# Self-attention with the values as stationary operand, probabilities divided by their sums before they are turned, and units of two even and two odd heads

## The chip, the cores and the metric

The kernel runs on one core of a Trainium2 chip. The time is device time of one execution, in microseconds (us). TensorE is called PE here (PEld are its weight loads), VectorE is DVE, ScalarE is ACT, GpSimd is POOL, and SP issues DMAs.

## What is computed

A decoder of seven stages on x of 32 samples, 112 rows and 256 columns, all in fp32. The change touches the first stage alone, self-attention with 8 heads of 64 columns on the normalised x:

```python
qk = x @ W_qk + b_qk
q, k = (qk[..., 0], qk[..., 1])
v = (x @ W_v + b_v).reshape(b, s, H, D_HEAD)
sim = jnp.einsum('bihd,bjhd->bhij', q, k) * scale
attn = jax.nn.softmax(sim, axis=-1)
o = jnp.einsum('bhij,bjhd->bihd', attn, v)
y = _layernorm(o @ W_out + b_out, ln_gamma, ln_beta)
return (y + x) * RSQRT2
```

The six stages behind it (projection of a context, two cross-attentions, two mixtures of experts, a gated attention) are the same before and after.

## The kernel before

`self_attention` (line 449) works in eight **groups** of four samples. Each sample is two **units** (u = 0 to 7 in a group, 64 in all); a unit is four heads, the even ones of a sample in an even unit and the odd ones in an odd unit. The order of work on each engine is written out by hand in `group` of that engine (PE line 613, ACT 676, DVE 761). Engines wait for each other by counting semaphores, and each engine works strictly in its own order. The first and the last group are written out; the six between run in a loop, where the values waited for are worked out in registers.

What a unit goes through, step by step:

- PE `scores` (L573): four matmuls of 64 rows by 112 columns, in one PSUM bank for even units and another for odd ones. Even heads stand in partitions 0 to 63 of qT and kT, odd heads in 64 to 127. A unit before uses one of the halves.
- DVE `shift`: the maximum over the keys (L727) and the subtraction (L730).
- ACT `exp` (L662).
- PE `turn_prob` (L582): four transposes of the probabilities; ACT `copy_probT` (L667) brings them to SBUF.
- PE `values` (L593): probT is stationary (112 columns), v moving (64 columns and one of ones, which gives the row's sum).
- DVE `normalise`: reciprocal of that sum (L737) and the product (L740), into `sa_o`.
- once per sample, PE `turn_out` (L602, four transposes of `sa_o`), ACT `copy_oT` (L673), PE `project` (L609, four matmuls of 256 columns), DVE `keep_y` (L747 to L751: bias and statistics).

In unit u PE does: turn_prob(u), scores(u + 1), a job of the next group, values(u), a second job, then `turn_out` of the sample before where u is even and `project` where u is odd. The jobs (`PLAN`, line 458) make the next group's operands: the transposes of x in u = 1, q and k in u = 2 to 5, v in u = 6 and 7. The last group has no jobs. DVE normalises the next group's x (`norm`, L708) at the start of unit 0, and takes the statistics of the context (`context_stats`, L758) in even units. The next unit's turn_prob needs the probabilities of u + 1, so scores, shift and exp of u + 1 run while PE does the rest of unit u.

Of the kernel before, what the change touches and what calls it, by code (L numbers as in the profile page):

```python
# [448 lines left out]
def self_attention(e):  # L449
# [5 lines left out]
    SCORE = (bank[0], bank[1])  # L455
    TURNED, PV, OT, Y = bank[2], bank[3], bank[6], bank[7]
# [6 lines left out]
    with ExitStack() as st:  # L463
# [12 lines left out]
        v = sb("sa_v", [T, 2, GROUP, H, HD + 1])  # L476
# [3 lines left out]
        rinv = sb("sa_rinv", [T, 2, HU])  # L480
        o = sb("sa_o", [T, 2, H, HD])
# [19 lines left out]
        rinv_done = count("sa_rinv_done")  # L501
        o_ready = count("sa_o_ready")
        oT_ps, oT_ready = count("sa_oT_ps"), count("sa_oT_ready")
# [16 lines left out]
        with nc.Block() as block:  # L520
# [9 lines left out]
            def _(pe):  # L530
# [33 lines left out]
                def scores(g, r, u):  # L564
                    s, odd = divmod(u, 2)
# [4 lines left out]
                    for i in range(HU):  # L570
                        h = 2 * i + odd
                        p0 = HD * odd
                        last = pe.matmul(SCORE[odd][0:T, i * T:(i + 1) * T],  # L573
                                         qT[p0:p0 + HD, r, h // 2, s * T:(s + 1) * T],
                                         kT[p0:p0 + HD, r, h // 2, s * T:(s + 1) * T], start=True, stop=True)
# [9 lines left out]
                def values(g, r, u):  # L585
                    s, odd = divmod(u, 2)
# [10 lines left out]
                def turn_out(g, s):  # L597
                    pe.wait_ge(o_ready, ONE + g * UNITS + 2 * s + 2)
                    pe.wait_ge(oT_ready, ONE + g * GROUP + s)
                    ov = o[:, s % 2].rearrange("t h e -> t (h e)")  # L600
                    for k in range(4):
                        last = pe.transpose(OT[:, k * T:(k + 1) * T], ov[:, k * P:(k + 1) * P], ident[0:T, 0:T])  # L602
                    last.then_inc(oT_ps, 1)
# [1832 lines left out]
```

## Time and profile before

| | us |
|---|---|
| median of 3 runs | 3142.16 |
| lowest and highest run | 3135.05 and 3143.45 |
| the profiled execution | 3136.99, its span 3135.2 |
| attention part of the stage, first turn_prob to last matmul | 73.72 to 473.96 |

Over the whole span PE is busy for 88%, DVE 48%, ACT 36%, POOL 20%; the granted clock of PE is 0.91 of full speed on average. In rows of busy time by stretch the columns are: the stretch, its length, busy us of PE, PEld, DVE, ACT and POOL (with their records), PE's granted clock, the DMAs' share and GB/s. Times in rows are us from the start of the span, those called "mean" are ns. PE prints an fp32 matmul as two records and a transpose as one, so a unit's four score matmuls are x8. A record is longer than the distance to the next, since matmuls are pipelined: what a step costs PE is the distance from its start to the next step's start. Clock 1.00 stands for TensorE at 2.4 GHz, 0.50 for 1.2 GHz.

### The profile page before, as it was taken

The page shows a single profiled execution, that of the slowest core. Times are in us where ns is not written, and L with a number is a line of the kernel's source. Part 1 is how long each engine was busy: PE and PEld are TensorE (multiplying, and loading weights), DVE is VectorE, ACT ScalarE, POOL GpSimd, SP SyncE. Part 2 cuts the span into 40 slices and gives each one's busy share as a digit, 9 for nine tenths or more (in the row PEclk, how much of TensorE's full clock was granted, in tenths as well). Part 3 has the DMA queues.
Part 4 walks back from the last instruction along what each step waited for, and adds up shares of the span by engine and source line. Part 5 has one row for each costly group of instructions (what it writes and reads, how often), then busy time and mean ns, then how long its engine had stood idle before and what let it go on. Part 6 is the DMA issues. An engine that isn't in the chain of part 4 may idle for free. (4 is left out here: it accounts for less than half of the span.)

```text
span 3135.2 us, 58175 instructions
## 1 busy us (share of the span) xinstructions
PE 2746.9 (88%) x19352; PEld 2247.6 (72%) x19352; DVE 1498.8 (48%) x3187; ACT 1113.3 (36%) x2348; POOL 638.5 (20%) x660
## 2 busy tenths in 40 slices
PE   4999994996999998499999969899789999849992
PEld 2767672674888887488888857666578888848882
DVE  3455556335767664500000036555567777553334
ACT  1222235332555553033333324332145555402220
POOL 0000000003333331022222200000143333104542
PEclk8899996997999997599999989999889999859996
DMA  5000001786777772255655668600168888415666
GB/s 135 23 23 22 22 22 31 245 283 164 191 189 190 188 191 66 67 176 177 207 178 194 202 195 296 224 1 1 42 157 210 204 204 205 111 35 183 206 212 195
DMA packets 284132, 459.92 MB, mean 147 GB/s; under 512 B 73234, under 2 KB 211956, under 8 KB 284004
## 3 DMA queue, kind: packets, MB, share of 16 engines
q1 hardware_dynamic: 267236, 408.97, 46.0%
q0 software_dynamic: 16768, 49.30, 4.8%
q8 instruction: 72, 1.18, 0.2%
q14 instruction: 56, 0.46, 0.0%
HBM read 339.13 MB, written 119.02 MB: 146 GB/s over the span
## 5 line engine op out<-in xcount | busy, mean ns | idle before, releaser
L1389 ACT ACTIVATE x_probT<-banks 125x448 f32<-125x448 f32 x768 | 418.0, 544 | 402.3 <-PE banks L1292 392.6
L1495 DVE TENSOR_REDUCE x_neg_max<-banks 112x2 f32<-112x750 f32 x512 | 455.8, 931 | 97.7 <-PE banks L1276 97.7
L2000 PE MATMUL banks<-f_xT,f_w 128*128 128x256 f32 (+1 forms) x1680 | 368.7, 376 | 24.5 <-DMA f_b<-in_L_ffn_b 9.7
L2000 PEld LDWEIGHTS banks<-f_xT,f_w 128*128 128x128 f32 x1680 | 310.0, 196 | 76.6 <-issue 11.6
L1433 POOL TENSOR_TENSOR x_diag<-ident,x_neg_max 112x448 fp32r<-112x448 f32 x256 | 240.8, 941 | 575.4 <-DVE x_neg_max L1495 553.5
L2012 PE MATMUL banks<-f_w,f_hT 128*128 128x256 f32 x1584 | 354.3, 380 | 0.0
L1290 PE MATMUL banks<-x_diag,x_ones 112*125 112x448 f32 x768 | 324.5, 423 | 10.5 <-POOL x_diag L1433 9.8
L2012 PEld LDWEIGHTS banks<-f_w,f_hT 128*128 128x128 f32 x1584 | 296.2, 191 | 37.5
L1292 PEld LDWEIGHTS banks<-x_qP,x_kP 128*125 128x125 f32 x1536 | 291.3, 190 | 14.9
L1292 PE MATMUL banks<-x_qP,x_kP 128*125 128x224 f32 x1536 | 291.5, 271 | 0.0
L1276 PE MATMUL banks<-x_kP,x_qP 128*112 128x376 f32 x1024 | 264.5, 341 | 10.4 <-DMA x_qP<-q_halves 9.6
L2059 DVE TENSOR_TENSOR f_y<-banks,f_b 128x256 f32<-128x256 f32 x66 | 25.1, 420 | 478.2 <-PE banks L2012 478.2
L1940 POOL DMA_INDIRECT y_rows<-f_y,f_goes x132 | 131.2, 994 | 463.7 <-DVE f_y L2059 338.3
L2034 ACT ACTIVATE f_hT<-banks,f_b 128x256 f32<-128x256 f32 (+1 forms) x280 | 126.0, 461 | 219.7 <-PE banks L2000 202.2
L1308 PE MATMUL banks<-x_probT,x_v 125*32 125x112 f32 x6144 | 200.5, 263 | 0.8 <-ACT x_o4T L1397 0.8
L1931 POOL DMA_INDIRECT f_x_slots<-x_rows,f_came x132 | 130.2, 986 | 250.2 <-POOLq L101 198.7
L1290 PEld LDWEIGHTS banks<-x_diag,x_ones 112*125 112x125 f32 x768 | 143.8, 187 | 41.9 <-ACT x_probT L1389 22.0
L1308 PEld LDWEIGHTS banks<-x_probT,x_v 125*32 125x32 f32 x6144 | 138.7, 109 | 30.2 <-ACT x_o4T L1397 1.2
L1276 PEld LDWEIGHTS banks<-x_kP,x_qP 128*112 128x112 f32 x1024 | 147.9, 180 | 12.8 <-issue 10.1
L2037 ACT ACTIVATE f_hT<-banks 128x256 f32<-128x256 f32 (+1 forms) x140 | 52.0, 371 | 189.4 <-PE banks L2000 188.4
L949 PE MATMUL banks<-p_ctxT,x_wk_by_head 128*128 128x375 f32 x256 | 91.3, 501 | 27.2 <-DMA p_ctxT<-in_ctx_T 20.4
L2051 DVE TENSOR_TENSOR f_hT<-f_hT 128x256 f32<-128x256 f32 (+1 forms) x140 | 57.4, 410 | 90.7 <-ACT f_hT L2037 89.3
(321 smaller groups left out, 4096.7 us busy)
## 6 DMA issues: line engine op xcount, KB each, us to landing
x_kP<-k_halves SPq DMA_DIRECT2D x512, 188.0 KB, 3.6
f_w<-in_L_ffn_w SPq DMA_DIRECT2D x70, 1024.0 KB
f_w<-in_L_ffn_w SPq DMA_DIRECT2D x70, 512.0 KB
x_qP<-q_halves SPq DMA_DIRECT2D x512, 56.0 KB, 3.2
x_v<-v_rows SPq DMA_DIRECT2D x64, 408.0 KB, 3.2
k_halves<-p_halves SPq DMA_DIRECT2D x32, 752.0 KB, 3.6
k_halves<-f_d_halves SPq DMA_DIRECT2D x32, 752.0 KB, 4.0
q_halves<-x_q_halves SPq DMA_DIRECT2D x64, 224.0 KB, 2.3
```

The lines of the kernel that those rows point to most:

```text
L1276: last = pe.matmul(bank[2 * pair + k][0:T, 0:NKV + 1], qP[:, s, k, 2 * q + pair, :], kP[:, r, 2 * q + pair, :], start=True, stop=True)
L1290: pe.matmul(to, ones[:], diag[:, u % RING].rearrange("t h k -> t (h k)"), start=True, stop=False)
L1292: last = pe.matmul(to[:, 2 * pair * T:2 * (pair + 1) * T].rearrange("k (h t) -> k h t", t=T), kP[:, r, 2 * q + pair, keys], qP[:, s, :, 2 ...
L1308: last = pe.matmul(PV[j * VW:(j + 1) * VW, 0:T], v[0:KB, s % 2, at:at + VW], probT[:, u % 2, c, j, :], start=(c == 0), stop=(c == NJ - 1))
L1389: act.activation(probT[:, u % 2, c].rearrange("k h t -> k (h t)"), ST[i % 2][0:KB, 0:HU * T], ACT.Exp).then_inc(exp_done, 1)
L1433: pool.tensor_tensor(diag[:, u % RING], wide(ident[0:T, 0:T].unsqueeze(1), 1, HU), wide(mx[:, u % RING, :].unsqueeze(2), 2, T), ALU.mult). ...
L1495: dve.tensor_reduce(mx[:, u % RING, 2 * pair:2 * pair + 2], psum[0:T, 2 * pair:2 * pair + 2, 0:NKV], AX_X, ALU.max, negate=True).then_inc( ...
L1931: pool.indirect_dma_start(out=x_slots[:, n % 2, j, :], out_offset=None, in_=e.x_rows, in_offset=bass.IndirectOffsetOnAxis(ap=came[:, at:at ...
L1940: pool.indirect_dma_start(out=e.y_rows, out_offset=bass.IndirectOffsetOnAxis(ap=goes[:, at:at + 1], axis=0), in_=y[:, n % 2, j, :], in_off ...
L2000: last = pe.matmul(bank[1 + f % 3][:, 0:width], w1[:, r, k, f * P:(f + 1) * P], xT[:, r, k, 0:width], start=(k == 0), stop=(k == KD - 1))
L2012: last = pe.matmul(bank[4 + 2 * r + j][:, 0:D], hT[:, f, j * P:(j + 1) * P], w2[:, r, f, :], start=(f == 0), stop=(f == NF - 1))
L2034: act.activation(hT[:, f, 0:width], bank[1 + f % 3][:, 0:width], ACT.Gelu, bias=b1[:, r, f:f + 1]).then_inc(h_raw, 1)
```

## The change

- **Units** take another four heads: both even and both odd ones of half a sample (`part` 0 and 1), issued by turns: even, odd, even, odd. The scores of even heads go to bank 0, those of odd heads to bank 1, and the part selects columns 0 or 256 of both. DVE reads both banks with one instruction.
- **values** has v as the stationary operand (64 columns) and probT moving (112 columns). The output is already turned: an even head lands in PSUM partitions 0 to 63 and an odd one in 64 to 127, in two banks used by turns. `turn_out` and its semaphores are gone. ACT copies 128x224 a unit (`copy_oT`, once a unit in place of 128x448 once a sample).
- **The division** is done on the probabilities: `normalise` is gone, and DVE's new `weigh` takes the sum of each row (112x448 to 112x4), its reciprocal, and the product over 112x448, between exp and turn_prob. turn_prob waits for `weighed`, not for `exp_done`.
- **Order**: DVE does shift(u + 1), context_stats where u is even, weigh(u + 1), jobs, keep_y. ACT does copy_probT(u), exp(u + 1), copy_oT(u - 1), jobs. PE does `project` of the sample before in even units. v has no column of ones.

The core of the diff (renamed counters and declarations left out):

```diff
     SCORE, SCW = (bank[0], bank[1]), 256
@@ scores
-                    for i in range(HU):
-                        h = 2 * i + odd
-                        p0 = HD * odd
-                        last = pe.matmul(SCORE[odd][0:T, i * T:(i + 1) * T],
...
+                    for i in range(PAIR):
+                        for odd in range(2):
+                            at = part * SCW + i * T
+                            p0 = HD * odd
+                            last = pe.matmul(SCORE[odd][0:T, at:at + T],
+                                             qT[p0:p0 + HD, r, PAIR * part + i, s * T:(s + 1) * T],
+                                             kT[p0:p0 + HD, r, PAIR * part + i, s * T:(s + 1) * T],
+                                             start=True, stop=True)
@@ turn_prob
-                    pe.wait_ge(exp_done, ONE + g * UNITS + u + 1)
+                    pe.wait_ge(weighed, ONE + g * UNITS + u + 1)
@@ values
-                    pe.wait_ge(o_ready, ONE + g * UNITS + u)
-                    for i in range(HU):
-                        last = pe.matmul(PV[0:T, i * (HD + 1):(i + 1) * (HD + 1)],
-                                         probT[:, u % 2, i, :], v[:, r, s, 2 * i + odd, :], start=True, stop=True)
+                    pe.wait_ge(oT_ready, ONE + least(g * UNITS + u - 1))
+                    for i in range(PAIR):
+                        for odd in range(2):
+                            last = pe.matmul(PV[part][odd * HD:(odd + 1) * HD, i * T:(i + 1) * T],
+                                             v[:, r, s, 2 * (PAIR * part + i) + odd, :],
+                                             probT[:, u % 2, odd * PAIR + i, :], start=True, stop=True)
@@ project, and PE's group
-                    pe.wait_ge(oT_ready, ONE + g * GROUP + s + 1)
+                    pe.wait_ge(oT_ready, ONE + g * UNITS + 2 * s + 2)
...
                         if u % 2 == 0 and (u > 0 or not is_first):
-                            turn_out(g, u // 2 - 1)
-                        if u % 2 == 1 and (u > 1 or not is_first):
                             project(g, u // 2 - 1)
@@ ACT
+                def copy_oT(g, u):
+                    s, part = divmod(u, 2)
+                    act.wait_ge(pv_ps, ONE + g * UNITS + u + 1)
                     act.wait_ge(y_ps, ONE + least(g * GROUP + s - 1))
...
+                        if u > 0 or not is_first:
+                            copy_oT(g, u - 1)
                         if not last:
                             for j in PLAN.get(u, ()):
                                 job(g + 1, 1 - r, *j)
@@ DVE
+                def weigh(g, u):
+                    dve.wait_ge(exp_done, ONE + g * UNITS + u + 1)
+                    dve.tensor_reduce(total[:, u % 2, 0, :], prob[:, u % 2], AX_X, ALU.add).then_inc(summed, 1)
+                    dve.wait_ge(summed, ONE + (g * UNITS + u) * 2 + 1)
+                    dve.reciprocal(total[:, u % 2, 1, :], total[:, u % 2, 0, :]).then_inc(summed, 1)
+                    dve.wait_ge(summed, ONE + (g * UNITS + u) * 2 + 2)
+                    dve.tensor_tensor(prob[:, u % 2], prob[:, u % 2], wide(total[:, u % 2, 1, :].unsqueeze(2), 2, T),
+                                      ALU.mult).then_inc(weighed, 1)
...
-                        normalise(g, u)
+                        if u % 2 == 0:
+                            context_stats(g, u // 2)
+                        if u + 1 < UNITS:
+                            weigh(g, u + 1)
+                        elif not last:
+                            weigh(g + 1, 0)
                         if not last:
                             for j in PLAN.get(u, ()):
                                 job(g + 1, 1 - r, *j)
                         if u % 2 == 1 and (u > 1 or not is_first):
                             keep_y(g, u // 2 - 1)
-                        if u % 2 == 0:
-                            context_stats(g, u // 2)
```

**PE, units 2 and 3 of the first group**, before. L582 is turn_prob, L573 scores, L549 the q and k jobs, L593 values, L602 turn_out, L609 project:

```order
L582 MATMUL banks<-ident,sa_prob 112x112 x4
L573 MATMUL banks<-sa_kT,sa_qT 112x112 x4
L549 MATMUL banks<-sa_xnT,w_q 128x448 x2
L593 MATMUL banks<-sa_v,sa_probT 112x65 x4
L549 MATMUL banks<-sa_xnT,w_k 128x448 x2
L602 MATMUL banks<-ident,sa_o 128x112 x4
L582 MATMUL banks<-ident,sa_prob 112x112 x4
L573 MATMUL banks<-sa_kT,sa_qT 112x112 x4
L549 MATMUL banks<-sa_xnT,w_q 128x448 x2
L593 MATMUL banks<-sa_v,sa_probT 112x65 x4
L549 MATMUL banks<-sa_xnT,w_k 128x448 x2
L609 MATMUL banks<-w_o,sa_oT 112x256 x4
```

The same place after (L583 turn_prob, L548 jobs, L595 values, L604 project):

```order
L583 MATMUL banks<-ident,sa_prob 112x112 x4
L573 MATMUL banks<-sa_kT,sa_qT 112x112 x4
L548 MATMUL banks<-sa_xnT,w_q 128x448 x2
L595 MATMUL banks<-sa_probT,sa_v 64x112 x4
L548 MATMUL banks<-sa_xnT,w_k 128x448 x2
L604 MATMUL banks<-w_o,sa_oT 112x256 x4
L583 MATMUL banks<-ident,sa_prob 112x112 x4
L573 MATMUL banks<-sa_kT,sa_qT 112x112 x4
L548 MATMUL banks<-sa_xnT,w_q 128x448 x2
L595 MATMUL banks<-sa_probT,sa_v 64x112 x4
L548 MATMUL banks<-sa_xnT,w_k 128x448 x2
```

Four transposes a sample are gone, and project has moved from the odd unit to the even one before it.

**DVE, unit 0 of the first group**, before, with what each row waits for (L708 is norm, L727 and L730 shift, L737 and L740 normalise, L756 and L758 the context's statistics):

```order
L708 TENSOR_SCALAR sa_xn<-x_res,x_mean_var,x_rstd 112x256 x3
L727 TENSOR_REDUCE sa_max<-banks 112x4 [waits sa_scores_ps]
L730 TENSOR_TENSOR sa_prob<-banks,sa_max 112x448 [waits sa_probT_ps,sa_max_done]
L737 RECIPROCAL sa_rinv<-banks 112x4 [waits sa_pv_ps]
L740 TENSOR_TENSOR sa_o<-banks,sa_rinv 112x4x64 [waits sa_oT_ps,sa_rinv_done]
L756 MEMSET scratch 128x1 [waits sa_ctx_loaded0]
L758 BN_STATS context_stat<-sa_ctx_rows 125x6 x3
```

The same place after (L699 norm, L720 and L723 shift, L747 and L749 the context's statistics, L728 to L732 weigh):

```order
L699 TENSOR_SCALAR sa_xn<-x_res,x_mean_var,x_rstd 112x256 x3
L720 TENSOR_REDUCE sa_max<-banks 112x4 [waits sa_scores_ps]
L723 TENSOR_TENSOR sa_prob<-banks,sa_max 112x448 [waits sa_probT_ps,sa_max_done]
L747 MEMSET scratch 128x1 [waits sa_ctx_loaded0]
L749 BN_STATS context_stat<-sa_ctx_rows 125x6 x3
L728 TENSOR_REDUCE sa_total<-sa_prob 112x4 [waits sa_exp_done]
L730 RECIPROCAL sa_total<-sa_total 112x4 [waits sa_summed]
L732 TENSOR_TENSOR sa_prob<-sa_prob,sa_total 112x448 [waits sa_summed]
```

Two instructions that waited for values are gone; three that wait for exp, two of them for the one before, stand behind the context's statistics.

## Rows read from the trace of the kernel before

**Rows 1.** Busy time by stretch: the six loop groups, then the last group

```profile
124.97:438.99 314.02, 302.60 (x1586) 215.79 (x1584) 162.12 (x420) 89.72 (x168) 0.00 (x0) 0.92 0.08 22
438.99:473.96 34.97, 31.02 (x213) 25.34 (x211) 20.46 (x61) 10.65 (x20) 0.00 (x0) 0.95 0.06 17
```

**Rows 2.** Timeline of PE, two units at full clock: start, us, instructions

```profile
195.92 0.55 PE L602 MATMUL banks<-ident,sa_o 112*128 112x112 f32 x4
196.31 0.55 PE L582 MATMUL banks<-ident,sa_prob 112*112 112x112 f32 x4
196.78 1.03 PE L573 MATMUL banks<-sa_kT,sa_qT 64*112 64x112 f32 x8
197.75 1.77 PE L549 MATMUL banks<-sa_xnT,w_q 128*128 128x448 f32 x4
199.36 0.91 PE L593 MATMUL banks<-sa_v,sa_probT 112*112 112x65 f32 x8
200.10 1.72 PE L549 MATMUL banks<-sa_xnT,w_k 128*128 128x448 f32 x4
201.66 1.89 PE L609 MATMUL banks<-w_o,sa_oT 128*112 128x256 f32 x8
203.39 0.36 PE L582 MATMUL banks<-ident,sa_prob 112*112 112x112 f32 x2
```

**Rows 3.** Busy time by stretch: units 0 and 1 of a loop group

```profile
176.66:181.28 4.62, 2.83 (x26) 2.37 (x24) 4.05 (x13) 1.18 (x3) 0.00 (x0) 0.92 0.01 2
181.28:190.35 9.07, 9.07 (x37) 7.52 (x37) 2.54 (x7) 2.47 (x5) 0.00 (x0) 0.50 0.13 32
```

**Rows 4.** Timeline of PE, unit 1 at half clock

```profile
181.28 1.00 PE L582 MATMUL banks<-ident,sa_prob 112*112 112x112 f32 x4 [1.78 <-ACT sa_prob L662]
182.20 1.83 PE L573 MATMUL banks<-sa_kT,sa_qT 64*112 64x112 f32 x8
...
186.94 3.62 PE L609 MATMUL banks<-w_o,sa_oT 128*112 128x256 f32 x8
```

**Rows 5.** Timeline of DVE and ACT around unit 0 of the same group

```profile
175.13 0.69 DVE L720 COPY sa_v<-banks 112x512 f32<-112x512 f32 x1 [1.12 <-PE banks L560]
176.97 0.42 DVE L747 TENSOR_TENSOR sa_y<-banks,w_bo 112x256 f32 x1 [1.15 <-PE banks L609]
...
177.95 1.38 DVE L708 TENSOR_SCALAR sa_xn<-x_res,x_mean_var,x_rstd 112x256 f32 x4
179.25 0.62 DVE L727 TENSOR_REDUCE sa_max<-banks 112x4 f32<-112x448 f32 x1
179.99 0.62 DVE L730 TENSOR_TENSOR sa_prob<-banks,sa_max 112x448 f32<-112x448 f32 x1
180.53 0.17 DVE L737 RECIPROCAL sa_rinv<-banks 112x4 f32<-112x4 f32 x1
...
180.65 0.58 ACT L662 ACTIVATE sa_prob<-sa_prob 112x448 f32<-112x448 f32 x1 [2.86 <-DVE sa_prob L730]
```

**Rows 6.** Timeline of PE in the first cross-attention: matmuls of 32 stationary columns

```profile
801.29 0.78 PE L1308 MATMUL banks<-x_probT,x_v 125*32 125x112 f32 x24
802.00 0.36 PE L1258 MATMUL banks<-x_xnT,x_wq_by_head 128*128 128x112 f32 x1
```

**Rows 7.** Groups of instructions by form: busy us, mean ns

```profile
L1308 PE MATMUL banks<-x_probT,x_v 125*32 125x112 f32 x6144 | 200.5, 263 | 0.8 <-ACT x_o4T L1397 0.8
L1308 PEld LDWEIGHTS banks<-x_probT,x_v 125*32 125x32 f32 x6144 | 138.7, 109 | 30.2 <-ACT x_o4T L1397 1.2 <-issue 0.4
L2364 DVE TENSOR_TENSOR ga_aT<-ga_aT 112x448 f32<-112x448 f32 x8 | 4.9, 617 | 1.7 <-ACT ga_aT L2298 1.7
L1402 ACT ACTIVATE x_oT<-banks 128x224 f32<-128x224 f32 x32 | 11.4, 358 | 2.0 <-PE banks L1329 2.0
```

**Rows 8.** Busy time by stretch: the last group's unit 0, and its end

```profile
438.99:442.49 3.50, 2.83 (x26) 2.37 (x24) 2.79 (x9) 1.18 (x3) 0.00 (x0) 1.00 0.00 0
...
465.27:473.96 8.69, 7.41 (x32) 5.42 (x32) 2.14 (x8) 1.47 (x3) 0.00 (x0) 0.80 0.00 0
```

More of the change, by code:

```diff
@@ L454, in self_attention @@
     HU = H // 2
-    SCORE = (bank[0], bank[1])
-    TURNED, PV, OT, Y = bank[2], bank[3], bank[6], bank[7]
+    SCORE, SCW = (bank[0], bank[1]), 256
+    TURNED, PV, Y = bank[2], (bank[3], bank[6]), bank[7]
+    psum, PAIR = e.psum, 2
     JOB = (bank[4], bank[5])
@@ L475, in self_attention @@
         kT = sb("sa_kT", [P, 2, 4, GT])
-        v = sb("sa_v", [T, 2, GROUP, H, HD + 1])
+        v = sb("sa_v", [T, 2, GROUP, H, HD])
         mx = sb("sa_max", [T, 2, HU])
@@ L479, in self_attention @@
         probT = sb("sa_probT", [T, 2, HU, T])
-        rinv = sb("sa_rinv", [T, 2, HU])
-        o = sb("sa_o", [T, 2, H, HD])
+        total = sb("sa_total", [T, 2, 2, HU])
         oT = sb("sa_oT", [P, 2, 4, T])
@@ L500, in self_attention @@
         pv_ps = count("sa_pv_ps")
-        rinv_done = count("sa_rinv_done")
-        o_ready = count("sa_o_ready")
-        oT_ps, oT_ready = count("sa_oT_ps"), count("sa_oT_ready")
+        summed, weighed = count("sa_summed"), count("sa_weighed")
+        oT_ready = count("sa_oT_ready")
         y_ps, y_done = count("sa_y_ps"), count("sa_y_done")
@@ L564, in scores @@
                 def scores(g, r, u):
-                    s, odd = divmod(u, 2)
+                    s, part = divmod(u, 2)
                     if u == 0:
@@ L585, in values @@
                 def values(g, r, u):
-                    s, odd = divmod(u, 2)
+                    s, part = divmod(u, 2)
                     if u == 0:
@@ L626, in group @@
                         if u % 2 == 0 and (u > 0 or not is_first):
-                            turn_out(g, u // 2 - 1)
-                        if u % 2 == 1 and (u > 1 or not is_first):
                             project(g, u // 2 - 1)
                     if last:
-                        turn_out(g, GROUP - 1)
                         project(g, GROUP - 1)
@@ L668, in copy_probT @@
                                    ACT.Copy).then_inc(pT_ready, 1)
-                def copy_oT(g, s):
-                    act.wait_ge(oT_ps, ONE + g * GROUP + s + 1)
+                def copy_oT(g, u):
+                    s, part = divmod(u, 2)
+                    act.wait_ge(pv_ps, ONE + g * UNITS + u + 1)
                     act.wait_ge(y_ps, ONE + least(g * GROUP + s - 1))
-                    act.activation(oT[:, s % 2].rearrange("p a b -> p (a b)"), OT[:, 0:4 * T],
-                                   ACT.Copy).then_inc(oT_ready, 1)
+                    act.activation(oT[:, s % 2, PAIR * part:PAIR * (part + 1), :].rearrange("p a b -> p (a b)"),
+                                   PV[part][:, 0:PAIR * T], ACT.Copy).then_inc(oT_ready, 1)
                 def group(g, r, is_first, last):
@@ L685, in group @@
                                 job(g + 1, 1 - r, *j)
-                        if u % 2 == 0 and (u > 0 or not is_first):
-                            copy_oT(g, u // 2 - 1)
                     if last:
-                        copy_oT(g, GROUP - 1)
+                        copy_oT(g, UNITS - 1)
                 for jobs in PLAN.values():
@@ L725, in shift @@
                     dve.wait_ge(s_ps, ONE + g * UNITS + u + 1)
-                    sc = SCORE[u % 2][0:T, 0:HU * T].rearrange("t (h k) -> t h k", k=T)
-                    dve.tensor_reduce(mx[:, u % 2, :], sc, AX_X, ALU.max).then_inc(mx_done, 1)
+                    at = u % 2 * SCW
+                    sc = psum[0:T, 0:2, at:at + PAIR * T].rearrange("t o (i k) -> t o i k", k=T)
+                    m4 = mx[:, u % 2, :].rearrange("t (o i) -> t o i", o=2)
+                    dve.tensor_reduce(m4, sc, AX_X, ALU.max).then_inc(mx_done, 1)
@@ L784, in _ @@
                 shift(0, 0)
+                weigh(0, 0)
                 all_groups(dve, group)
```

24 lines of the change are left out of this document (2 added, 22 removed).

## The prediction

> **What bounds the kernel now.** I read the busy time by stretch first. The change sits in the attention part of stage one, 73.72 to 473.96 us, which is 400.2 us of the span. PE is busy for 302.60 of the 314.02 us of the loop's groups, while DVE has work for half of them [rows 1]. The part is bound by PE, with two exceptions. The timeline gives PE's steps at full clock, each from its start to the next one's [rows 2]: turn_out 0.39, turn_prob 0.47, scores 0.97, a q job 1.61, values 0.74, a k job 1.56, project 1.73. They add up without a gap to 5.74 for an even unit with q and k jobs, and 7.08 for an odd one.
>
> The first exception is unit 0 of a loop group. It lasts 4.62 with PE busy for 2.83 [rows 3], and PE ends it by waiting 1.78 for exp [rows 4], because DVE first does the next group's norm, 1.38 [rows 5]. Behind that wait the granted clock is 0.50 for the whole of unit 1, 9.07 us [rows 3]: scores take 1.83 and project 3.62 [rows 4], against 1.03 and 1.89 at full clock [rows 2]. By the steps, unit 1 at full clock is 0.47 + 0.97 + 0.74 + 1.73 + two short x transposes of 0.45 = 4.8, so a group at full clock would be about 48.8 and is 314.02/6 = 52.3. The low clock costs 3.5 a group. The second exception is the last group, which has no jobs: its unit 0 takes 3.50 with PE busy for 2.83 [rows 8], so it is bound by the loop scores, shift, exp, turn_prob. The group takes 34.97 at a mean clock of 0.95 [rows 1].
>
> **PE's steps after.** No row shows the score pairs in two row halves. The nearest one is matmuls in four column quarters: 24 records start within 0.78 - 0.26 = 0.52 (a record lasts 0.26 [rows 7]), and the next line starts 0.19 after the last of them [rows 6]. That is six rounds of four, 0.10 a round; one record of the same 112 moving columns, alone in the array, takes about as long (0.97 for 8). So tiles in different parts of the array run together. Scores after: four rounds of two, three steps of 0.10, 0.19 to leave, and 0.09 for the first load, as now: 0.57. If row halves did not run together, it stays at 0.97. Values after, in two column halves: 0.30 + 0.19 + 0.10 to enter = 0.60; if they did not, 0.97, since 112 columns move and not 65. I take 0.57 and 0.60: the row of four quarters is the same machine and the same kind of matmul. turn_out goes: 0.39 a sample. turn_prob, the jobs and project stay.
>
> The Trainium skill, "TensorE: Matmul & The Clock Gate", section "Part 3: Packing small matmuls", says that a weight load overlaps matmuls in flight only when its row group differs. That favours the scores and speaks against the values, whose two halves share all row groups. By it the four quarters would show their loads one after the other, 24 times the mean load of 0.109 [rows 7], 2.6 us; the line takes 0.71 [rows 6]. The trace disagrees, so values keep 0.60; by the rule they would take about 0.97, and the total would be some 15 us more.
>
> **DVE's steps after.** Out: reciprocal and product over 112x256, which no one on PE's path waited for except turn_out. In: weigh, on the path between exp and turn_prob. Sum over 112x448: not shown from SBUF; the maximum over the same shape from PSUM takes 0.62 [rows 5]. Reciprocal 0.17 [rows 5]. Product over 112x448: 0.617 from SBUF [rows 7]. With 0.04 between dependent ones: 0.66 + 0.21 + 0.66 = 1.53. In the loop the value of each wait is computed in a register between them: shift's two halves start 0.74 apart though the first takes 0.62 [rows 5], so 0.08 more for each of two waits: 1.7. Bounds: a sum twice as cheap gives 1.4, twice the register time 1.9. The context's statistics (1.0, even units) now stand between shift and weigh; exp (0.58) hides the first 0.6, the rest adds 0.4. Behind weigh's waits on DVE are queued the k and v copies and keep_y; PE needs them a unit later, and that covers them.
>
> So the shortest unit is: turn_prob 0.48, scores 0.57 and 0.1 to DVE, shift 1.32, exp 0.63, weigh 1.53, **4.6** (4.9 in the loop, 5.1 to 5.3 with the statistics). It was 3.5 [rows 8].
>
> **The sum, at full clock.** Units 2 to 7 of a group with jobs: PE's work falls by 0.40 + 0.14 a unit and 0.39 a sample, 6 x 0.54 + 3 x 0.39 = 4.4. Project now lies in even units, which become 0.47 + 0.57 + 1.6 + 0.60 + 1.55 + 1.73 = 6.5, and odd ones 4.8; both are at or above the new loop, so PE still bounds them, odd ones barely. Unit 0 of a loop group: DVE does the v copy (0.69), keep_y (0.9), norm (1.38), shift, context and weigh in a row, all behind PE's last v job: 0.1 + 0.6 + 0.9 + 1.3 + 1.4 + 1.0 + 1.7 = 7.0, where it was 4.6. PE can't fill it: project needs copy_oT of unit 7, which ACT does behind exp(1) (0.36 for 128x224 [rows 7]), so PE waits for 3.5 us ahead of project. Unit 1: 4.9, as before. Net -4.4 + 2.4 = -2.0 a group at full clock.
>
> **The clock.** PE's wait in unit 0 doubles from 1.8 to 3.5 us, so I expect the same fall to 0.50, earlier, and full clock again only after PE has been busy through about as long a stretch as now (9.07 us, rows 3). At half clock: project of unit 0, +1.7; turn_prob and scores of unit 1, +1.0; then half of unit 2's work before the clock is back, +2.2. That is 4.9 against 3.5 now: -2.0 + 1.4 = -0.6 for each of six groups, **-3.6**. The first group, 73.72 to 124.97, has no project in unit 0: 51.3 becomes 50, **-1.3**.
>
> **The last group.** Full clock would give units of 5.1 and 4.6, 39.5 with the tail against 34.97, +4.5. But PE's work for a sample is 2 x (0.48 + 0.57 + 0.60) + 1.73 = 5.0 of 9.7 us, 52%. Unit 0 of a loop group fell to half clock with 2.83 of 4.62 busy, 61% with the tails of records counted [rows 3]; the last group of now holds full clock with 31.02 of 34.97 busy [rows 1] until its end, where the clock is 0.80 on average [rows 8]. I take it that the clock falls at the start of the last group and stays. Then an odd unit is 4.6 + 0.48 + 0.57 = 5.7. An even one is bound by PE with project behind copy_oT: 0.96 + 1.14 + 0.1 + 1.3 + 0.63 + 0.4 = 4.5, then project 3.4, 7.9. Four of each are 54.4, **+19.4**.
>
> Together -3.6 - 1.3 + 19.4 = **+14.5** us. Against the profiled execution's 3136.99 that is 3151.5. The median of the runs is 5.2 above the profile; I give half of that and forecast **3154**. The other stages are not touched.
>
> **Rivals.** (A) The clock holds in the last group, or is soon back. For it: the last group of now drops PE to 81% in every other unit without losing it [rows 8]. Then -4.9 + 4.5 = 0: 3137 to 3144. (B) Row halves do not run together, the scores stay at 0.97. Nothing in the trace shows a row half next to another. It adds 0.40 to 36 PE-bound units of the groups with jobs and six more of the first, 17 us, and 0.4 (0.8 at half clock) to the remaining 22, which have scores on their loop, 14 us: 3185. (C) The other side, faster: the clock does not fall in unit 0 either. Then each loop group takes 52.3 - 3.5 - 2.0 = 46.8, -5.5 x 6, the first -5, the last +4.5: -33, 3109. It decides by whether the records of unit 0, in tiles side by side, keep the clock up over a gap of 3.5 us; against it stands that 1.8 us without work were enough to lose it [rows 4]. (D) Column halves do not run together, or weigh costs the upper bound of 1.9: values 0.97 in 64 units, up to +20, 3170.
>
> **Chances.** Forecast 0.55 (3146 to 3164), A 0.17, B 0.13, C 0.07, D 0.08. The likeliest gives 3154. The range, down to where A ends with cheaper waits and up to nearly B: 3128 to 3184. About 0.3% (9.4 us) is what a measurement of this kernel can tell from no change. Slower by more than that: most of the forecast's case, B and D, 0.60. Within: A and the low end of the forecast, 0.29. Faster: C and the low end of A, 0.11.
>
> **What would show it.** Eight records of scores in 0.57 and of values in 0.60, distance to the next step. Unit 0 of a loop group 7 to 8.7 us with an idle stretch on PE ahead of project, released by ACT's copy. Odd units at 4.8, even ones at 6.5. The last group at 0.50 with units of 5.7 and 7.9. It is wrong if scores keep 0.97, if the last group runs at 1.00, or if weigh takes much more or less than 1.6.

## The result, and the profile after

| | kernel before | changed kernel |
|---|---|---|
| median of 11 runs each | 3139.51 us (3134.08 to 3143.56) | 3153.03 us (3145.76 to 3156.87) |
| profiled execution, span | 3135.2 us | 3155.2 us |
| mean granted clock of it | 0.909 | 0.899 |

The changed kernel takes 1.0036 times as long, with a 95% interval of 1.0028 to 1.0044: 13.5 us slower by the medians. The forecast was 3154.

Busy time by stretch, changed kernel, in the columns of [rows 1]: units 0 to 3 of the second loop group, then the first group, the six loop groups and the last group.

```profile
173.14:182.04 8.90, 5.28 (x29) 3.74 (x28) 6.13 (x17) 1.36 (x3) 0.00 (x0) 0.74 0.13 35
182.04:187.54 5.50, 3.71 (x30) 2.72 (x28) 2.73 (x6) 2.23 (x5) 0.00 (x0) 0.80 0.00 0
187.54:195.79 8.25, 8.25 (x36) 5.04 (x37) 4.81 (x13) 2.00 (x4) 0.00 (x0) 0.79 0.13 35
195.79:200.69 4.90, 4.90 (x30) 2.68 (x28) 2.67 (x5) 1.89 (x4) 0.00 (x0) 1.00 0.02 5
75.00:121.56 46.56, 43.21 (x240) 25.74 (x241) 30.12 (x71) 14.72 (x31) 0.00 (x0) 0.89 0.10 26
121.56:435.99 314.43, 275.07 (x1489) 164.43 (x1488) 195.14 (x468) 89.66 (x192) 0.00 (x0) 0.90 0.08 23
435.99:488.70 52.71, 36.63 (x193) 25.93 (x191) 26.05 (x68) 10.70 (x24) 0.00 (x0) 0.64 0.04 11
```

Against [rows 1]: PE is busy in the loop groups for 275.07 us where it was 302.60, and yet they take the same 314. The 27.5 us of work that the change takes from PE come back as waits and as low clock. The last group takes 52.71 where it was 34.97. The attention part's last matmul ends 14.7 us later (488.70 against 473.96). The other 5.3 us of the spans' difference of 20.0 lie behind it, in work that the change doesn't touch. The profiled execution is the slowest of the changed kernel's 11 runs, so its stretches are at the upper end; how far they move from run to run is seen in e1.

### The profile page after: what moved, and what is told of

It is laid out like the page before. It is cut to its first block and busy times, and to the rows that moved or that the text cites. A ratio compares the mean times of both kernels' runs of the same rounds, so it can differ in the third digit from the quotient of the medians.

```text
span 3155.2 us, 58021 instructions
## 1 busy us (share of the span) xinstructions
PE 2724.9 (86%) x19224; PEld 2193.7 (70%) x19224; DVE 1543.8 (49%) x3250; ACT 1113.8 (35%) x2380; POOL 637.4 (20%) x660
## 5 line engine op out<-in xcount | busy, mean ns | idle before, releaser
L604 PE MATMUL banks<-w_o,sa_oT 128*112 128x256 f32 x256 | 80.2, 469 | 32.9 <-ACT sa_oT L666 32.9
```

## The steps in the trace after

Timeline of PE, changed kernel: unit 0's wait for oT, the end of unit 1, then a pair of steps at full clock.

```profile
178.49 3.76 PE L604 MATMUL banks<-w_o,sa_oT 128*112 128x256 f32 x8 [3.37 <-ACT sa_oT L666]
182.04 0.95 PE L583 MATMUL banks<-ident,sa_prob 112*112 112x112 f32 x4
182.93 1.09 PE L573 MATMUL banks<-sa_kT,sa_qT 64*112 64x112 f32 x8
...
187.54 0.93 PE L583 MATMUL banks<-ident,sa_prob 112*112 112x112 f32 x4 [1.79 <-DVE sa_prob L732]
...
196.27 0.65 PE L573 MATMUL banks<-sa_kT,sa_qT 64*112 64x112 f32 x8
196.85 1.77 PE L548 MATMUL banks<-sa_xnT,w_q 128*128 128x448 f32 x4
198.55 0.60 PE L595 MATMUL banks<-sa_probT,sa_v 112*64 112x112 f32 x8
199.08 1.40 PE L548 MATMUL banks<-sa_xnT,w_k 128*128 128x448 f32 x3
```

Scores take 196.85 - 196.27 = 0.58 from start to start, 0.97 before [rows 2]. Values take 199.08 - 198.55 = 0.53, 0.74 before; the q job ahead of them lasts 1.70 instead of 1.61, so entering the column halves costs 0.09 there, and values are 0.62 together. Project of unit 0 waits 3.37 us for copy_oT and then runs at half clock, 3.55 from start to start. That is the wait that the prediction put ahead of project at 3.5. Units 3 and 4 take 4.90 and 6.62 (195.79, 200.69, 207.31); the steps of the prediction gave 4.8 and 6.5.

Timelines of DVE and ACT, changed kernel: weigh in unit 1, then exp and copy_oT in unit 0.

```profile
185.99 0.62 DVE L728 TENSOR_REDUCE sa_total<-sa_prob 112x4 f32<-112x448 f32 x1 [0.64 <-ACT sa_prob L654]
186.64 0.18 DVE L730 RECIPROCAL sa_total<-sa_total 112x4 f32<-112x4 f32 x1
186.86 0.62 DVE L732 TENSOR_TENSOR sa_prob<-sa_prob,sa_total 112x448 f32<-112x448 f32 x1
...
177.62 0.58 ACT L654 ACTIVATE sa_prob<-sa_prob 112x448 f32<-112x448 f32 x1 [3.35 <-DVE sa_prob L723]
178.10 0.34 ACT L666 ACTIVATE sa_oT<-banks 128x224 f32<-128x224 f32 x1
```

Weigh takes 187.54 - 185.99 = 1.55 us on the path from exp to turn_prob. Copy_oT starts only when ACT is done with exp of the next unit, which had itself waited 3.35 us for DVE.

One thing in this trace was in nobody's sum. Timeline of DVE, changed kernel, where the loop goes into its second pass (its body holds two groups):

```profile
225.93 0.43 DVE L742 BATCH_NORM_STATS2 sa_y_stat<-sa_y  x1
229.54 1.38 DVE L699 TENSOR_SCALAR sa_xn<-x_res,x_mean_var,x_rstd 112x256 f32 x4 [3.19 <-issue]
```

DVE does nothing for 3.19 us, and waits for nobody. At 337.00, where the third pass begins, it is 3.05. In the kernel before, the same two places show 0.41 and 0.37. The two groups that begin there have a unit 0 of 12.19 and 12.05 us, where the other four have 8.90 to 8.99.

## Experiments

Each is compared with the kernel before on the same chip (about 3139.5 us), unless it says otherwise. The ratio is to the kernel before.

**e1: the score matmuls in another order.** The two row halves are both in a unit, but no longer by turns.

```diff
-                    for i in range(PAIR):
-                        for odd in range(2):
+                    for odd in range(2):
+                        for i in range(PAIR):
```

> The changed kernel with the four score matmuls of a unit in the order even, even, odd, odd instead of by turns; nothing else differs. My theory, that neighbours in two row halves run together: the step of the scores goes from 0.58 us back to 0.87 to 0.97 (only the second and third can still meet), which adds 12 to 17 us in the 42 units that PE bounds and 6 to 14 us in the 22 that have the scores on their loop: 3171 to 3184 against 3153. Rival, that the scores were never side by side and the shorter step has another cause, such as the two banks: the step stays at 0.58 and the time at 3153.

Measured: 3151.95 us (3141.59 to 3158.84), ratio 1.0038 [1.0025, 1.0052], the same as the changed kernel. Timeline of PE, e1:

```profile
200.13 0.65 PE L573 MATMUL banks<-sa_kT,sa_qT 64*112 64x112 f32 x8
200.72 1.02 PE L548 MATMUL banks<-sa_xnT,w_q 128*128 128x448 f32 x2
```

The step is still 0.59. That row halves must alternate was wrong, and the 3171 to 3184 with it.

This kernel has the changed kernel's steps and its median, but here the profile caught its fastest run. That shows how much the same steps can differ in time. Busy time of the six loop groups, e1:

```profile
123.96:428.44 304.48, 264.63 (x1489) 156.94 (x1488) 195.32 (x468) 89.56 (x192) 0.00 (x0) 0.94 0.09 23
```

They take 304.48 us where the changed kernel's profile has 314.43, at a granted clock of 0.94 instead of 0.90. Unit 2 takes 6.68 us in three of the groups and 8.27 or 8.28 in the other three; in the changed kernel's profile it takes 6.68 in one, 8.21 to 8.26 in four and 9.71 in one. The last matmul of the attention part ends at 481.25, 7.3 us later than before the change and not 14.7.

Whether it is the halves that shorten the step, or the two banks of PSUM that they write to, was left to e5.

**e5: two banks, one row half.** The kernel before, with the four score matmuls of a unit written to two banks by turns.

```diff
-                        last = pe.matmul(SCORE[odd][0:T, i * T:(i + 1) * T],
+                        at = odd * SCW + i // 2 * T
+                        last = pe.matmul(SCORE[i % 2][0:T, at:at + T],
```

> The kernel before with its units of four even or four odd heads, all scores in one row half as before, but written to two banks by turns (head 0 and 2 to bank 0, 1 and 3 to bank 1). It parts the two things that changed at once in the scores. If the row halves make the step short, it stays at 0.97 us here and the time at 3139. If the second bank does, it falls to 0.58 and the time to about 3104, as with units of mixed heads.

Measured: 3138.17 us, one run. Timeline of PE, e5:

```profile
203.77 1.03 PE L575 MATMUL banks<-sa_kT,sa_qT 64*112 64x112 f32 x8
204.74 0.64 PE L550 MATMUL banks<-sa_xnT,w_q 128*128 128x448 f32 x1
```

The step stays at 0.97, so it is the row halves that run together, whatever the order within a unit. Whether they also would with both halves written to one bank wasn't tried.

**e4: mixed head units alone.** The kernel before with units of two even and two odd heads. Division, turn_out and the values stay as they were.

```diff
-                    for i in range(HU):
-                        h = 2 * i + odd
-                        p0 = HD * odd
-                        last = pe.matmul(SCORE[odd][0:T, i * T:(i + 1) * T],
+                    for i in range(PAIR):
+                        for odd in range(2):
+                            at = part * SCW + i * T
+                            p0 = HD * odd
+                            last = pe.matmul(SCORE[odd][0:T, at:at + T],
```

> The kernel before with one part of the change alone: units of two even and two odd heads, whose score matmuls are issued by turns into two banks. Values, normalise and turn_out are as before, no weigh. My theory: scores 0.58 instead of 0.97 in all units, 0.4 in each of 42 units that TensorE bounds and a part of it in the last group, with some of it given back to the clock: 3139 falls to 3115 to 3128. Rival, that what side by side scores save is taken back by waits for exp, since TensorE gets to turn_prob sooner: 3133 to 3142.

Measured: 3103.97 us (3101.56 to 3106.05), ratio 0.9882 [0.9866, 0.9899]. Busy time by stretch, e4: units 0 and 1 of a loop group, the six loop groups, the last group.

```profile
168.51:173.13 4.62, 2.48 (x25) 1.98 (x24) 4.05 (x13) 1.17 (x3) 0.00 (x0) 1.00 0.01 2
173.13:179.19 6.06, 6.06 (x36) 5.17 (x37) 2.54 (x7) 2.47 (x5) 0.00 (x0) 0.72 0.16 48
120.98:407.42 286.44, 272.94 (x1586) 188.15 (x1584) 158.47 (x420) 89.24 (x168) 0.00 (x0) 0.96 0.09 24
407.42:438.42 31.00, 27.09 (x213) 21.52 (x211) 20.36 (x61) 10.65 (x20) 0.00 (x0) 1.00 0.07 20
```

This part of the change is worth 36 us by itself. That is 11 us beyond the fast end of what was expected, and more than the steps' 0.40 in each of 64 units (26 us). The rest is low clock given back: unit 1 takes 6.05 or 6.06 in each of the six groups, at 0.72, where it took 7.77 to 9.07 and 9.07 at 0.50 in the group of [rows 3]. The last group, 31.00, keeps the full clock.

**e2: weigh left out.** The changed kernel without the division by the row sums (its output lacks it). Turn_prob waits for exp, as before the change.

```diff
-                    pe.wait_ge(weighed, ONE + g * UNITS + u + 1)
+                    pe.wait_ge(exp_done, ONE + g * UNITS + u + 1)
...
-                        if u + 1 < UNITS:
-                            weigh(g, u + 1)
-                        elif not last:
-                            weigh(g + 1, 0)
```

> The changed kernel with the division of the probabilities left out: no sum, reciprocal and product on VectorE, turn_prob waits for exp; the attention's rows are then not divided by their sums. It prices weigh on the path between exp and turn_prob. My theory: units without jobs are bound by scores, shift, exp, weigh, turn_prob, so a unit of the last group falls from 4.9 at full clock and 5.5 at half clock to 3.2 or 4, unit 0 of a loop group from 8.9 to about 6, and the waits of TensorE shrink with it: 3105 to 3118. Rival, that weigh hides beside the jobs and the loss is all from project standing behind copy_oT: units with q and k jobs and the last group's even units stay as they are (7.8), within 12 us of 3153.

Measured: 3114.18 us (3111.18 to 3118.7), ratio 0.9921 [0.9904, 0.9937]. Busy time by stretch, e2: units 0 and 1, the loop groups, the last group; then the start of project in a unit 0, from PE's timeline.

```profile
166.02:174.81 8.79, 5.17 (x29) 3.64 (x28) 4.82 (x14) 1.36 (x3) 0.00 (x0) 0.81 0.12 35
174.81:178.00 3.19, 2.80 (x30) 2.04 (x28) 1.81 (x5) 1.17 (x3) 0.00 (x0) 0.98 0.00 0
118.61:404.20 285.59, 260.14 (x1490) 154.99 (x1489) 129.97 (x324) 88.45 (x192) 0.00 (x0) 0.96 0.09 25
404.20:445.65 41.45, 30.14 (x193) 21.42 (x191) 16.46 (x46) 10.70 (x24) 0.00 (x0) 0.75 0.05 14
...
219.31 3.65 PE L602 MATMUL banks<-w_o,sa_oT 128*112 128x256 f32 x8 [3.90 <-ACT sa_oT L664]
```

Leaving weigh out gains 39 us, most of it in unit 1 (3.19 instead of 5.50), in unit 2 (6.68 instead of 8.25) and in the last group (41.45 instead of 52.71). Not all of it is weigh's time on the path: DVE's two stops at the loop's branch, 6.2 us together in the changed kernel, are 0.8 here (e11 and e12 say why). But unit 0 stays at 8.8, not 6 as expected: PE still waits there 3.9 us for copy_oT. So unit 0 of the changed kernel isn't set by weigh but by the place of copy_oT behind exp.

**e6: copy_oT ahead of exp.** The changed kernel with ACT's two steps exchanged.

```diff
                         copy_probT(g, u)
+                        if u > 0 or not is_first:
+                            copy_oT(g, u - 1)
                         if u + 1 < UNITS:
                             exp(g, u + 1)
                         elif not last:
                             exp(g + 1, 0)
-                        if u > 0 or not is_first:
-                            copy_oT(g, u - 1)
```

> The changed kernel with ScalarE's copy_oT(u - 1) ahead of exp(u + 1) instead of behind it. My theory now: unit 0 of a loop group (8.9 us) is long because project waits for that copy, so project starts at 1.7 in place of 5.3 and the unit ends with weigh at 6.7; the last group's even units go from 7.8 to about 6.6. Some of it goes to a low clock that comes a unit later: 3130 to 3138 against 3153. Rival: the same wait moves behind project to turn_prob, which weigh releases, and the clock falls as before: 3147 to 3156.

Measured: 3125.14 us (3121.7 to 3130.0), ratio 0.9957 [0.9941, 0.9974]. PE's timeline of a unit 0 in e6, and its busy time with that of the last group:

```profile
173.72 1.98 PE L604 MATMUL banks<-w_o,sa_oT 128*112 128x256 f32 x8
178.49 0.59 PE L583 MATMUL banks<-ident,sa_prob 112*112 112x112 f32 x4 [2.79 <-DVE sa_prob L732]
```

```profile
171.80:178.49 6.69, 3.64 (x29) 2.55 (x28) 6.13 (x17) 1.37 (x3) 0.00 (x0) 1.00 0.05 9
423.33:463.65 40.32, 28.82 (x193) 20.78 (x191) 26.01 (x67) 10.72 (x24) 0.00 (x0) 0.79 0.06 15
```

Project now runs at once, and at full clock (1.98 instead of 3.76). Unit 0 falls from 8.90 to 6.69, the last group from 52.7 to 40.3. Two exchanged steps of ACT are 28 us, where 15 to 23 were expected (3130 to 3138). What is left of unit 0 is the wait for weigh.

**e7: and norm behind weigh.** e6, with DVE's norm of the next group moved from the head of unit 0 to behind its weigh.

```diff
-                        if u == 0 and not last:
-                            norm(g + 1)
...
                             weigh(g + 1, 0)
+                        if u == 0 and not last:
+                            norm(g + 1)
```

> As the kernel before it in this call, and VectorE normalises the next group's x behind weigh in unit 0 instead of ahead of shift. My theory: unit 0 loses the 1.4 us of norm as well, 5.4 in place of 6.7, TensorE's wait there shrinks below what cost the clock, and a loop group takes 47 to 48.5: 3112 to 3124. Rival: the transposes of x in unit 1 wait for norm instead and the clock falls there, 3130 or more.

Measured: 3115.3 us (3113.33 to 3120.41), ratio 0.993 [0.9913, 0.9946]; unit 0 is 5.34 (170.29 to 175.63). With copy_oT and norm out of the way the changed kernel is still 11 us slower than e4, which has neither weigh nor the shorter values. (e4 still has norm at the head of unit 0. Against e8 below, where norm is moved too, e7 is 27 us slower.)

**e3: PE filled with work that nobody reads.** The changed kernel with matmuls added where PE waits, seven in unit 0, and in the last group four and six a unit.

```diff
+                def fill(n):
+                    for k in range(n):
+                        pe.matmul(JOB[0][0:T, 0:D], w.q[:, k % 2, 0:T], w.o[:, k % 4, :], start=True, stop=True)
...
+                        if u == 0 and not last:
+                            fill(7)
+                        elif last:
+                            fill(4 if u % 2 == 0 else 6)
```

> The changed kernel with matmuls of 256 columns whose result no one reads put into TensorE's waits: 7 behind the values of unit 0 in groups with jobs, and in the last group 4 in even and 6 in odd units, all written to a bank that is free there. Work is added, none taken out. My theory, that the low clock and not the waits alone makes the last group and units 0 to 2 long: the clock stays at 1.00, loop groups take 46.5 to 47.5 instead of 52.4, the last group 40 to 42 instead of 53: 3100 to 3112. Rival, that the waits themselves are the cost and the clock follows them at no price: the same or longer, 3150 to 3165.

Measured: 3134.78 us (3126.35 to 3138.39), ratio 0.9978 [0.9966, 0.999]. Busy time by stretch, e3: unit 2 of a loop group, the last group.

```profile
186.09:194.40 8.31, 8.31 (x37) 4.96 (x37) 4.83 (x13) 2.00 (x4) 0.00 (x0) 0.79 0.14 37
427.83:469.70 41.87, 40.38 (x273) 30.23 (x271) 26.03 (x67) 10.71 (x24) 0.00 (x0) 1.00 0.05 15
```

With more work the last group takes 41.87 at full clock instead of 52.71 at 0.64. Six of the added matmuls (12 records), 2.7 us, stand between its last values and its last project, so without them it is 39.2: the forecast's 39.5 for this group at full clock. In the loop's groups without a stop of DVE, units 0 and 1 now keep the full clock (7.18 and 4.64 at 1.00), but it is low in part of unit 2, behind the wait of unit 1. So the run missed its 3100 to 3112.

**e9: unit 1 filled too.** e3 with three more such matmuls in unit 1 (all of them now write the other job bank).

```diff
+                        elif u == 1 and not last:
+                            fill(3)
```

> The changed kernel with matmuls no one reads in TensorE's waits, as in the third kernel of the first call, and 3 more behind the values of unit 1 in groups with jobs, where the clock still fell there. If the low clock is what is left of the loss in the loop groups, they take 46.5 to 47.5 us (full clock by the steps: 46.4) in place of 50.7: 3106 to 3116. If a wait is paid at its length whatever the clock, 3130 or more.

Measured: 3125.58 us (3119.16 to 3128.03), ratio 0.9954 [0.9938, 0.9971]. Busy time by stretch, e9: a loop group at full clock, and one that begins at the loop's branch.

```profile
122.26:169.68 47.42, 46.24 (x270) 28.25 (x269) 32.52 (x78) 14.98 (x32) 0.00 (x0) 1.00 0.09 26
216.92:267.26 50.34, 46.23 (x269) 28.25 (x268) 32.58 (x78) 14.98 (x32) 0.00 (x0) 1.00 0.08 23
```

At full clock a loop group takes 47.42, of which unit 0 is 7.26 and unit 1 4.73; the forecast had 7.0, 4.9 and 46.8 in all. In the other group unit 0 is 10.18: DVE's stop shows here without any low clock. The group that begins at the loop's next branch takes 52.01, with a unit 0 of 11.82. The median is 10 us above the upper end of what was expected. The profiled execution spans 3117.4, so this one trace doesn't show where the other runs lost the rest. The low clock costs the changed kernel 27 us or more, since e9 does more work than it.

**e10: the kernel before, filled.** Four such matmuls in unit 0 of the kernel before.

```diff
+                        if u == 0 and not last:
+                            fill(4)
```

> The kernel before with 4 matmuls of 256 columns that no one reads behind turn_out in unit 0 of groups with jobs, in TensorE's wait of 1.8 us there; nothing is taken out. It prices the low clock of the kernel before, 3.5 us a group by the prediction: unit 1 falls from 8 to 9 us to 4.9, 3139 to 3113 to 3119. If the low clock costs nothing that counts: 3139 or more.

Measured: 3111.2 us (3109.68 to 3112.93), ratio 0.9908 [0.9891, 0.9924]. Busy time by stretch, e10: units 0 and 1, then the six loop groups.

```profile
172.41:177.03 4.62, 4.57 (x33) 3.65 (x31) 4.04 (x13) 1.17 (x3) 0.00 (x0) 1.00 0.01 2
177.03:181.83 4.80, 4.80 (x36) 4.19 (x37) 2.54 (x7) 2.37 (x5) 0.00 (x0) 1.00 0.25 60
123.82:416.65 292.83, 291.74 (x1633) 205.91 (x1632) 162.14 (x420) 89.15 (x168) 0.00 (x0) 1.00 0.09 24
```

Work that nobody reads makes the kernel 28 us faster, 2 us beyond the fast end of what was expected. In the two traces the attention part, up to the end of its last matmul, is 24.0 us shorter, where seven groups at the prediction's 3.5 are 24.5. Unit 0 is as long as before, 4.62, with PE busy for 4.57 of it instead of 2.83, and unit 1 takes the 4.80 that the prediction's steps gave it, instead of 9.07 [rows 3] (7.77 to 9.07 in the six groups). A loop group is 48.8, as worked out.

**e8: the version that the readings point to.** e4, with DVE's norm moved behind the normalise of unit 0, so that shift, exp and turn_prob come first.

```diff
-                        if u == 0 and not last:
-                            norm(g + 1)
...
                         normalise(g, u)
+                        if u == 0 and not last:
+                            norm(g + 1)
```

> The kernel before with the scores' part of the change alone, as the fourth kernel of the first call, and norm behind normalise in unit 0. My theory: unit 0 of a loop group goes from 4.6 to 3.5 and TensorE's wait from 1.9 to 0.8, so the clock no longer falls in unit 1: 1.1 and 1.5 us less in each of seven groups, 3104 falls to 3084 to 3092. Rival: the transposes of x wait for norm in unit 1 and it comes to the same, 3100 to 3106.

Measured: **3088.72 us** (3088.28 to 3089.97), ratio 0.9839 [0.9823, 0.9856], 51 us faster than before and the fastest of all. Busy time by stretch, e8: units 0 and 1, the six loop groups.

```profile
166.68:169.94 3.26, 2.48 (x26) 1.98 (x24) 2.69 (x8) 1.17 (x3) 0.00 (x0) 1.00 0.00 0
169.94:174.91 4.97, 4.47 (x36) 3.80 (x37) 3.77 (x12) 2.35 (x5) 0.00 (x0) 1.00 0.22 60
121.69:392.09 270.40, 263.47 (x1585) 179.61 (x1584) 157.51 (x420) 88.69 (x168) 0.00 (x0) 1.00 0.09 26
```

The clock stays at full through the loop. A group is 45.1 us.

**e11 and e12: DVE's stop at the branch.** e11 is e8 with more DVE instructions and little more work. e12 is e2 with more work for DVE and few more instructions (like e2 it leaves the division out). Of both, one run each.

```diff
                         normalise(g, u)
+                        for k in range(6):
+                            dve.memset(spare[:, 6 * (u % 2) + k:6 * (u % 2) + k + 1], 0.0)
```

> The fastest kernel so far (e8) with six one-column writes to a spare tile added on DVE in each unit; nothing reads them. DVE's instructions in the loop body become more than in the changed kernel (e8's body has 226 rows of instructions, the changed kernel's 273, this one over 300), while DVE's work grows by about 0.5 us a unit only. Theory (length): DVE's stop of 3 us at the loop's branch, seen in the changed kernel at 229.54 and 337.00, comes from the number of DVE instructions in the loop body. Then DVE's first work after each of the two branches stands behind 3 us of issue, and the time is 3096 to 3104. Rival (work): the stop comes from what DVE has been doing ahead of the branch; then it stays near 0.4 us and the time is 3089 to 3098.

```diff
+                    for k in range(2):
+                        s4 = spare[:, 2 * (u % 2) + k, :].rearrange("t (o i) -> t o i", o=2)
+                        dve.tensor_reduce(s4, sc, AX_X, ALU.max)
                     dve.tensor_reduce(m4, sc, AX_X, ALU.max).then_inc(mx_done, 1)
```

> The changed kernel without weigh (e2: the division by the row sums is left out) with two more maxima over the same scores in each unit, whose results nobody reads: DVE is busy for 1.3 us more a unit, and that stands on the path from scores to turn_prob as weigh does, but its loop body has 209 rows of instructions where the changed kernel's has 273 and e2's 193. Theory (length): no stop at the branch, 0.4 us of issue as in e2, and the time is between e2's 3114 and the changed kernel's 3152, less some 6 us: 3130 to 3146. Rival (work): the stop of 3 us is back at both branches.

Timeline of DVE at the start of the loop's second pass, e11:

```profile
210.63 0.43 DVE L762 BATCH_NORM_STATS2 sa_y_stat<-sa_y  x1
213.73 0.62 DVE L736 TENSOR_REDUCE sa_max<-banks 112x4 f32<-112x448 f32 x1 [2.67 <-issue]
```

And the same place, e12:

```profile
223.28 0.43 DVE L735 BATCH_NORM_STATS2 sa_y_stat<-sa_y  x1
224.12 1.38 DVE L698 TENSOR_SCALAR sa_xn<-x_res,x_mean_var,x_rstd 112x256 f32 x4 [0.42 <-issue]
```

Busy time of the six loop groups, e11, then e12:

```profile
119.73:401.98 282.25, 271.13 (x1585) 185.68 (x1584) 159.76 (x708) 88.83 (x168) 0.00 (x0) 0.96 0.09 25
119.42:431.28 311.86, 274.24 (x1489) 162.19 (x1488) 180.73 (x420) 88.83 (x192) 0.00 (x0) 0.91 0.08 23
```

e11 takes 3102.53 us and has the stop, 2.67 and, at 309.97, 2.60. e12 has it at neither place (0.4 each), though DVE is busy for 180.73 us in its loop groups and for only 159.76 in those of e11. So the stop comes with the number of instructions in DVE's loop body, not with its work. The loop makes three passes, so a body has a third of DVE's records in these rows. Bodies of 108 records (e2) and 140 (the kernel before, e4, e5, e8, e10, e12) are free of the stop, those of 156 (the changed kernel, e1, e3, e6, e7, e9) and 236 (e11) have it. Where between 140 and 156 it begins wasn't tried. The counts in the expectations are of another kind, rows of the program in which repeats share a row (the 32 maxima that e12 adds to a body are 16 of them), and no trace shows them. In e11 each stop also costs clock in the unit behind it (8.33 and 8.14 us instead of 4.77). Units 0 and 1 of these two groups are together 12 us longer than in e8, of the 14 us by which e11 is slower. e12's time, 3152.26, is outside its 3130 to 3146: maxima of 1.1 to 1.2 us on the path bring back all that leaving weigh out (1.55 us) had gained, by the same wait and low clock (unit 0 is 9.96 at 0.70).

## Why the prediction was right, point by point

- **PE's steps.** Scores 0.57 forecast (its terms 0.30, 0.19 and 0.09 add up to 0.58), 0.58 measured; values 0.60, and 0.62 with what entering costs the job ahead. Both were taken from the row of four column quarters [rows 6], and that row carried over to row halves and column halves alike. e5 shows that the row halves do it. That matmuls in column halves run together (eight records in 0.53 us) also speaks, as [rows 6] did, against the rule of the Trainium skill ("TensorE: Matmul & The Clock Gate", "Part 3: Packing small matmuls") that a weight load overlaps only matmuls of another row group. The same section of the Trainium skill also has loads into a background weight buffer pulled ahead of matmuls in flight, which the prediction left out. By that the loads of column halves could pass too; no run here tests it.
- **Weigh.** 1.53 from the rows, 1.7 taken for the loop, 1.55 measured. The 0.08 for each register value that was added weren't there.
- **Unit 0.** Forecast: PE waits 3.5 us for copy_oT, 7.0 at full clock (e9: 7.26), 8.7 with project at half clock (8.90). e2 and e6 show that this wait is ACT's order, as the prediction said, and that weigh has no part in it. The 7.0 itself was added up along another path, DVE's row of work that ends with weigh. That path is real, and e6, where it ends the unit, shows it at 6.69. But in the changed kernel project, behind copy_oT, ends later and so ends the unit. In e9, at full clock, weigh is done at 176.31, while project starts at 175.04 and lets turn_prob begin at 176.85. The two paths are half a microsecond apart there, and the sum was right although it was made on the shorter one.
- **The clock.** It fell in unit 0 and was back in unit 2, as forecast. Price of the low clock in a group, by the units of the changed kernel and of e9: 8.90 - 7.18, 5.50 - 4.65 and 8.25 - 6.67 are 4.2 us, 4.9 forecast. It isn't a fixed price: by unit 2 alone it is anything from 0 (6.68) to 3.0 us (9.71) in one and the same run, and e1's profile, with three such units at 6.68, has 10 us less in its loop groups.
- **The loop groups.** A group without a stop takes 51.6 (121.56 to 173.14), against 51.7 forecast and 52.3 before. But six of them were to gain 3.6 us and in this profile gained nothing (314.43 against 314.02). What the sum lacks is a term for DVE's stop, which makes unit 0 longer by 3.3 and 3.2 us in the groups that take 54.73 (224.54 to 279.27) and 52.45 (332.14 to 384.59). In the second of them the clock was back earlier (unit 1 at 4.97, unit 2 at 6.68), which hides most of it. The group between them takes 52.87, because the clock came back later in its unit 2; no row says why. Over all six that makes 4.2 us more than six times 51.7. In e1's profile the same six groups gain 9.5 us in spite of the two stops, so the 3.6 lies between two executions and neither confirms it.
- **The first group** was to take 50 from 73.72 on and gain 1.3. Its first turn_prob comes 1.3 later, behind the first weigh, which no step priced, and it then takes 46.56: 3.4 gained together.
- **The last group.** 54.4 forecast with the clock down throughout, 52.7 measured at a mean of 0.64. The clock is down in units 2, 4 and 6 (7.80 at 0.50 each), but it comes back for a part of every odd unit (0.81 to 0.85), which the prediction didn't expect. Odd units take 4.9 to 5.5 (5.7 forecast), even ones 7.2 to 7.8 (7.9). Rival A, that the clock holds here as it did in [rows 8], is out. e3 shows that A's 39.5 us was the right size for its case.
- **Together.** -3.6 - 1.3 + 19.4 = +14.5 was forecast. Measured are +0.4 in the loop groups, -3.4 in the first and +17.7 in the last, +14.7. So the sum is right partly because the missing term in the loop (+4.0) was offset by the first and the last group, each some 2 us less than forecast. With e1's profile the sum would be -9.5 - 1.0 + 17.8 = +7.3, the missing term and all, because there the clock was back sooner. The medians, 13.5 apart, lie between, and that the forecast of 3154 is within 1 us of 3153.03 is luck: single runs of the changed kernel lie up to 11 us apart. What is shown is the direction and the last group's share, which both profiles have at 17.7 to 17.8. The forecast's half of the 5.2 us gap to the median changes nothing: either way it lies within the runs.

What the prediction didn't price is what its parts are worth alone. The mixed units bring 36 us (e4). The other two parts, with their waits, take 49 us away again (e4 against the changed kernel). Of these 28 hang on ACT's order (e6). The stops of DVE, 3 us each, are part of the rest.

## What to carry to other kernels

Before a step is put on the path of a unit that has little PE work, look at the granted clock of the units behind it: a wait that loses the clock costs again there, and the cheapest remedy is the order of the helpers (the copy that PE needs next ahead of the one it needs later), or even matmuls that nobody reads. When a change has several parts, price each alone: here one part of it, with one DVE step moved, gives 3088.7 us, while the whole is slower than before.

## What the runs showed of the hardware that was not expected

- Four unread matmuls in a wait of 1.8 us make a kernel of 3139.5 us 28 us faster (e10), because the unit behind the wait keeps full clock: 4.80 instead of 7.77 to 9.07.
- Score matmuls in two row halves take 0.58 instead of 0.97 a step whether the halves alternate or come two and two (e1). Two PSUM banks without row halves give nothing (e5).
- DVE stops for 2.6 to 3.2 us at the loop's branch when its loop body has 156 or more records of instructions, and for 0.4 or less when it has 140 or fewer (e11, e12). What it does in the stop, no run shows.
- Two kernels of the same steps and the same median take 304.5 us (e1) and 314.4 (the changed kernel) for the six loop groups in their profiled executions. The difference is in when the granted clock comes back: unit 2 takes 6.68, about 8.3 or 9.71 us.
